# Another order of work at the opening of a three-layer kernel, and whole broadcasts of the group weights in place of pieces

## The reference

```python
x = x + 0.5 * ffn(layernorm(x)); x = x + attn(layernorm(x)); x = x + 0.5 * ffn(layernorm(x))

def ffn(x):                                   # 8 groups of 8 experts, inner width 352
    scores = softmax(x @ gate_w.T)            # 64 experts
    flat = w_e[:, inv_map]                    # the 8 best scores of each token, zero elsewhere
    scalar = flat.sum(-1)                     # one weight for each token and group
    soft = softmax(where(flat == 0, -1e9, flat), axis=-1)
    xg = x[:, None, :] + einsum('ngi,ghi->ngh', soft, mask_up_w)
    a = silu(einsum('ngh,gih->ngi', xg, gate_proj_w)) * einsum('ngh,gih->ngi', xg, up_proj_w)
    return einsum('ng,ngh->nh', scalar, einsum('ngi,ghi->ngh', a, down_proj_w))
```

## Time and profile before

| | |
|---|---|
| median of 3 runs | 1814.61 us |
| the profiled execution | 1818.04 us |
| its span, first to last instruction | 1816.3 us |
| PE busy | 1797.7 us, 99% |
| DVE busy | 876.9 us, 48% |
| ACT busy | 511.4 us, 28% |
| POOL busy | 174.2 us, 10% |
| moved by DMA | 384.13 MB, 211 GB/s on average |

### The profile page before, as it was taken

How to read it: one execution, slowest core, us unless ns; L and a number is a source line. 1 busy time by engine, 2 the same in 40 slices (tenths; PEclk the granted TensorE clock), 3 DMA queues, 4 the chain that set the end, 5 groups by cost and what they waited for, 6 DMA issues and landing times.

```text
span 1816.3 us, 21921 instructions
## 1 busy us (share of the span) xinstructions
PE 1797.7 (99%) x8320; PEld 1498.8 (83%) x8320; DVE 876.9 (48%) x1632; ACT 511.4 (28%) x754; POOL 174.2 (10%) x305
## 2 busy tenths in 40 slices
PE   7999999999999999999999999999999999999999
PEld 6888878888888888888888888888888888888887
DVE  6667454565445663343353656354664333422222
ACT  4334223532125431112212533114432111211111
POOL 2221210001100110000110101000101000000000
PEclk9999999999999999999999999999999999999999
DMA  5997765466465556567756556574466467656664
GB/s 202 366 354 261 278 228 170 159 200 209 139 220 199 173 185 197 184 235 236 243 182 203 190 189 225 166 236 160 155 203 219 145 237 255 223 173 229 234 232 167
DMA packets 108329, 384.13 MB, mean 211 GB/s; under 512 B 15520, under 2 KB 23584, under 8 KB 87488
## 3 DMA queue, kind: packets, MB, share of 16 engines
q1 hardware_dynamic: 65232, 278.36, 44.1%
q10 hardware_dynamic: 28816, 47.20, 9.1%
q0 software_dynamic: 14176, 57.16, 8.2%
HBM read 323.55 MB, written 41.81 MB: 201 GB/s over the span
## 4 chain that ended last, share of the span: by engine, by line
PE 92%; DMA 4%; DVE 2%; issue 0%; ACT 0%; SPq 0%; ACTq 0%; POOL 0%; DVEq 0%; POOLq 0%
PE bank L1243 27%; PE bank L1244 27%; PE bank L1245 27%; PE bank L1457 4%; DMA wt<-scr_w 2%; DMA b_all<-wgu 1%; PE bank L1396 1%; PE bank L1395 1%; PE bank L1388 1%; PE bank L1382 1%; DVE tb L865 1%; PE bank L1439 0%; PE bank L1438 0%; DVE o_all L860 0%; PE bank L1291 0%
## 5 line engine op out<-in xcount | busy, mean ns | idle before, releaser
L1243 PE MATMUL bank<-x_hi,wt 128*128 128x512 f32 x1328 | 521.0, 392 | 3.1 <-DMA wt<-scr_w 3.0
L1244 PE MATMUL bank<-x_hi,wt 128*128 128x512 f32 x1328 | 517.3, 390 | 0.0
L1245 PE MATMUL bank<-x_lo,wt 128*128 128x512 f32 x1328 | 517.3, 389 | 0.0
L808 DVE TENSOR_TENSOR act_t<-bank,sig 128x512 f32<-128x512 f32 x176 | 121.6, 691 | 514.9 <-PE bank L1457 473.9
L1243 PEld LDWEIGHTS bank<-x_hi,wt 128*128 128x128 f32 x1328 | 249.5, 188 | 55.4 <-DMA wt<-scr_w 4.8
L1245 PEld LDWEIGHTS bank<-x_lo,wt 128*128 128x128 f32 x1328 | 249.4, 188 | 52.0
L1244 PEld LDWEIGHTS bank<-x_hi,wt 128*128 128x128 f32 x1328 | 249.5, 188 | 50.3
L1243 PE MATMUL bank<-dt,a_hi 128*128 128x512 f32 x704 | 276.9, 393 | 0.8 <-issue 0.4
L1244 PE MATMUL bank<-dt,a_lo 128*128 128x512 f32 x704 | 274.4, 390 | 0.0
L1245 PE MATMUL bank<-dt,a_hi 128*128 128x512 f32 x704 | 274.2, 390 | 0.0
L722 ACT ACTIVATE sig<-bank 128x512 f32<-128x512 f32 x176 | 105.3, 598 | 559.7 <-PE bank L1457 559.6
(11 more groups left out here) (190 smaller groups left out, 1654.3 us busy)
## 6 DMA issues: line engine op xcount, KB each, us to landing
wt<-scr_w SPq DMA_DIRECT2D x140, 1152.0 KB, 5.2
dt<-scr_d SPq DMA_DIRECT2D x140, 512.0 KB, 5.3
s_bc<-scr_s ACTq DMA_DIRECT2D x128, 256.0 KB, 5.1
state<-wat POOLq DMA_DIRECT2D x28, 512.0 KB, 6.0
scr_w<-wt POOLq DMA_DIRECT2D x12, 1024.0 KB, 8.1
b_all<-wgu SPq DMA_DIRECT2D x22, 512.0 KB, 8.2
scr_d<-dt POOLq DMA_DIRECT2D x22, 512.0 KB, 5.0
x_lo<-tb SPq DMA_DIRECT2D x44, 256.0 KB, 5.1
```

The lines of the kernel that those rows point to most:

```text
L808: return nc.vector.tensor_tensor(dst, a, b, op)
L1243: mm(dst, wh, xh, start=start, stop=False)
L1244: mm(dst, wl, xh, start=False, stop=False)
L1245: return mm(dst, wh, xl, start=False, stop=stop)
```

## The change

Six things are done:

1. `first_norm` on ACT goes; `norm` on DVE normalises the first block's tiles too, with the same layout in memory as before. `first_scales` on POOL is replaced by `rstd_of`, and the shift is not computed. DVE's opening mixes statistics, normalisation and low parts.
2. The low part of gate_s moves from DVE to POOL.
3. `gu_hi(0)` and `gu_lo(0)` stand ahead of the masks' parts (mup); the preparation of fold_m stands ahead of the last `first_low`.
4. On PE, the first half of the gate sums of chunk 0 replaces the first half of `masked(0)` ahead of the fold; the second half of the sums follows the fold, then the whole of `masked(0)`.
5. `masked(4)` stands ahead of `down(0)`.
6. s_bc has two slots for each half of the groups. `load_s(half, m)` copies one group's row over all 128 partitions, 8 transfers in a phase where there were 28. A chunk that straddles two groups multiplies in parts, one for each group's partitions; a range from 32 to 128 is cut at 64. Over the 176 chunks that is 240 multiplications instead of 176.

```diff
-            def first_norm(i):
-                act.wait_ge(shift_ok, i + 1)
-                act.wait_ge(ld_x0[i], 16)
-                wait(act, xT_ok, i - 1)
-                nc.scalar.activation(xn[:, i % 2, :].rearrange("p (k d j) -> p k j d", k=KC, j=NQ),
-                                     xr(0)[:, i, :].rearrange("p (k j d) -> p k j d", k=KC, j=NQ), ACT.Identity,
-                                     bias=shift[:, i:i + 1], scale=rstd[:, i:i + 1]).then_inc(xn_ok, 1)
...
             def norm(r, i, src):
                 dve.wait_ge(mv_ok, r * NT + i + 1)
                 dve.wait_ge(rstd_ok, r * NT + i + 1)
+                if r == 0:
+                    wait(dve, xT_ok, i - 1)
+                    nc.vector.tensor_scalar(xn[:, i % 2, :].rearrange("p (k d j) -> p k j d", k=KC, j=NQ),
+                                            src[:, i, :].rearrange("p (k j d) -> p k j d", k=KC, j=NQ), mv[:, i, 0:1],
+                                            rstd[:, i:i + 1], ALU.subtract, ALU.mult).then_inc(xn_ok, 1)
+                    return
...
-            first_scales()
+            rstd_of(LN_R[0])
+            pool.wait_ge(gate_hi_ok, 1)
+            nc.gpsimd.tensor_tensor(gate_s[:, :, E:2 * E], raw_gate, gate_s[:, :, 0:E].bitcast(F32), ALU.subtract).then_inc(gate_ok, 1)
...
+            def s_number(n, g):
+                p, i = n // CH, g % (G // 2)
+                return p * (G // 2) + (G // 2 - 1 - i if p % 2 else i)
+            def s_last(n):
+                now = {s_number(n, g) for g, _, _ in group_rows(chunk(n))}
+                return sorted(now if n + 2 >= (n // CH + 1) * CH else now - {s_number(n + 2, g) for g, _, _ in group_rows(chunk(n + 2))})
+            def s_parts(c):
+                return [(g, a, b) for g, r0, r1 in group_rows(c) for a, b in (((32, 64), (64, P)) if (r0, r1) == (32, P) else ((r0, r1),))]
...
-            def load_s(n):
-                p, c = n // CH, chunk(n)
-                if n % CH < 2:
+            def load_s(half, m):
+                p, i = m // (G // 2), m % (G // 2)
+                if i == 0:
                     act.wait_ge(st_s, 16 * (p + 1))
-                for g, r0, r1 in group_rows(c):
-                    act.dma_start(s_bc[r0:r1, n % 2, :], scr_s[p % 2, g, :].partition_broadcast(r1 - r0)).then_inc(s_in[n % 2], 16)
+                g = half * (G // 2) + (G // 2 - 1 - i if p % 2 else i)
+                act.dma_start(s_bc[:, half, m % 2, :], scr_s[p % 2, g, :].partition_broadcast(P)).then_inc(s_in[half][m % 2], 16)
...
-                    if n + 2 < PHASES * CH:
-                        load_s(n + 2)
+                    for m in s_last(n):
+                        if m + 2 < PHASES * (G // 2):
+                            load_s(chunk(n) % 2, m + 2)
...
-                tt(act_t[:], s_bc[:, n % 2, :], act_t[:], ALU.mult).then_inc(t2_ok, 1)
+                for g, r0, r1 in s_parts(c):
+                    ins = tt(act_t[r0:r1, :], s_bc[r0:r1, c % 2, s_number(n, g) % 2, :], act_t[r0:r1, :], ALU.mult)
+                ins.then_inc(t2_ok, 1)
...
-            pe.wait_ge(setup_lo, 2)
-            masked(0, 0, KC // 2)
+            pe.wait_ge(gu_lo_ok, 1)
+            main(GB, 0, 0, 0, 0, KC // 2)
             pe.wait_ge(fold_ok, 1)
             router(0, 39)
-            masked(0, KC // 2, KC)
-            main(GB, 0, 0, 0)
+            main(GB, 0, 0, 0, KC // 2, KC)
+            pe.wait_ge(setup_lo, 2)
+            masked(0)
...
                     if n == 3:
+                        masked(4)
                         pe.wait_ge(sig_ok, 3)
                         pe.wait_ge(t1_ok, 3)
                         down(0)
-                        masked(4)
                         down(1)
```

More of the change, by code:

```diff
@@ L84, in build @@
         softT = sb("softT", [P, 2, 2, NB], F32R)
-        s_bc = sb("s_bc", [P, 2, NB])
+        s_bc = sb("s_bc", [P, 2, 2, NB])
         a_hi = sb("a_hi", [P, 2, NT, NQ, Q], F32R)
@@ L200, in build @@
         m_mm, m_raw_ok, m_top_ok, m_ok = (sem(n) for n in ("m_mm", "m_raw_ok", "m_top_ok", "m_ok"))
-        s_in, st_s = [sem(f"s_in{i}") for i in range(2)], sem("st_s")
+        s_in, st_s = [[sem(f"s_in{h}_{i}") for i in range(2)] for h in range(2)], sem("st_s")
         pool_init, setup_hi, setup_lo = (sem(n) for n in ("pool_init", "setup_hi", "setup_lo"))
@@ L424, in gu_lo @@
                                         ALU.subtract).then_inc(gu_lo_ok, 1)
[L426 to L436, removed]
             def store_w(c):
@@ L741, in _ @@
             act.dma_start(rank[:, 0, :], c_rank.partition_broadcast(P)).then_inc(ld_perm, 16)
[L742 to L743 removed]
             first_hi(0)
[L745 to L747 removed]
             act.wait_ge(ld_gate, 16)
             copy(gate_s[:, :, 0:E], raw_gate).then_inc(gate_hi_ok, 1)
+            first_hi(1)
             first_hi(2)
+            gu_hi(0)
             first_hi(3)
@@ L755, in _ @@
                      raw_mup[:, :, half, :].unsqueeze(2).broadcast_to([P, KC, 3, HE])).then_inc(setup_hi, 1)
-            gu_hi(0)
             gu_hi(1)
@@ L773, in _ @@
             m_top(1)
-            load_s(0)
+            for half in range(2):
+                load_s(half, 0)
             router(0, 49)
             router(0, 50)
-            load_s(1)
+            for half in range(2):
+                load_s(half, 1)
             for p in range(PHASES):
@@ L1150, in gate @@
                 dve.wait_ge(t1_ok, n + 1)
-                dve.wait_ge(s_in[n % 2], s_fill(n))
-                tt(act_t[:], s_bc[:, n % 2, :], act_t[:], ALU.mult).then_inc(t2_ok, 1)
+                c = chunk(n)
+                for g, _, _ in group_rows(c):
+                    m = s_number(n, g)
+                    dve.wait_ge(s_in[c % 2][m % 2], 16 * (m // 2 + 1))
+                for g, r0, r1 in s_parts(c):
+                    ins = tt(act_t[r0:r1, :], s_bc[r0:r1, c % 2, s_number(n, g) % 2, :], act_t[r0:r1, :], ALU.mult)
+                ins.then_inc(t2_ok, 1)
             def rest_a(n):
@@ L1169, in first_stats @@
                 stats_of(LN_R[0], i, xr(0))
-            for i in range(NT):
-                first_stats(i)
-            for i in range(NT):
-                first_low(i)
-                if i == 1:
-                    dve.wait_ge(gate_hi_ok, 1)
-                    tt(gate_s[:, :, E:2 * E], raw_gate, gate_s[:, :, 0:E].bitcast(F32), ALU.subtract).then_inc(gate_ok, 1)
-            dve.wait_ge(setup_hi, 2)
-            for half in range(2):
-                mp = mup[:, half, :, :].rearrange("p k (r e) -> p k r e", r=4)
-                tt(mp[:, :, 3, :], raw_mup[:, :, half, :], mp[:, :, 0, :].bitcast(F32), ALU.subtract).then_inc(setup_lo, 1)
-            gu_lo(0)
+            first_stats(0)
+            first_stats(1)
+            norm(LN_R[0], 0, xr(0))
+            first_stats(2)
+            norm(LN_R[0], 1, xr(0))
+            first_stats(3)
+            for i in range(NT - 1):
+                first_low(i)
+                if i < 2:
+                    norm(LN_R[0], i + 2, xr(0))
             dve.wait_ge(ld_perm, 48)
@@ L1191, in _ @@
             nc.vector.tensor_scalar(fold_m[:, E:2 * E], perm_w[:], iota[:, 0:1], None, ALU.is_equal).then_inc(fold_ok, 1)
+            first_low(NT - 1)
+            gu_lo(0)
+            dve.wait_ge(setup_hi, 2)
+            for half in range(2):
+                mp = mup[:, half, :, :].rearrange("p k (r e) -> p k r e", r=4)
+                tt(mp[:, :, 3, :], raw_mup[:, :, half, :], mp[:, :, 0, :].bitcast(F32), ALU.subtract).then_inc(setup_lo, 1)
             gu_lo(1)
@@ L1428, in weights, with masked @@
                 return hi, lo
-            def masked(c, k0=0, k1=KC):
+            def masked(c):
                 pe.wait_ge(gu_lo_ok, c + 1)
```

18 lines of the change are left out of this document (4 added, 14 removed).

## The result

The changed kernel takes 1818.7 us, the median of 20 executions (1816.15 to 1820.7), against 1814.92 for the kernel before (20 executions, 1813.36 to 1817.65). The ratio is 1.0017, with a 95% interval of 1.0011 to 1.0023: 2.0 to 4.2 us more, where 0.5 more was forecast and 1812.3 to 1817.4 was the range. The kernel is slower, by little: the ratio says 3.1 us, the medians 3.8, and the interval excludes that nothing changed.

A forecast was written before the change was run, and what follows sets the result against it. PE bounds the kernel, busy 1797.7 of 1816.3 us. Terms +0.9 (opening), +1.8 (masked(4)), -1.0 (77 us), -1.2 (weights) and 0 (multiplications) give +0.5 on the median 1814.6: 1815.1 us, range 1812.3 to 1817.4.

The forecast's parts named there:

- the two reliefs: PE's wait at 77.57 us and its waits for weights from scratch: forecast -1.0 and -1.2 us.
- step 1: Opening up to the fold, then the router's chain: PE stands from 33.8 to 35.5 us; cost +0.9 us.
- step 2: masked(4) ahead of down(0): PE waits for chunk 4's low weights from 47.54 to 49.94; +1.8 us, ends 0 and +2.0.
- The duration d: Opening: time of one tile's normalisation on DVE, taken as 1.1 us, with ends 0.55 and 1.29.
- the rival of the quick normalisation: Opening: DVE takes 0.55 to 0.7 us a tile, giving -1.0 instead of +0.9; 1813.2 us, chance 0.25.
- 9.0 + 4d: Opening: time in us when the fourth normalisation on DVE ends; 13.4 us with 1.1 us a tile.
- -1.0 at 77 us: PE's wait for sig of chunk 5 at 77.57 us disappears: -1.0 us, ends 0 and -1.0.
- -1.2 for the weights: PE's three waits for scratch weights: 0.7 off the longest, the other two gone; ends 0 and -3.0 us.
- the transfers were the whole cause: Rival: all 3.0 us of PE's waits for weights go, giving 1813.3 us; chance 0.10.
- The multiplications in parts: 64 more multiplications on DVE at straddling chunks: 44 us of DVE work hidden behind PE, cost 0.

The follow-up runs named there:

- the whole broadcasts alone: Kernel before with only the s_bc change: one group's row copied over all partitions per transfer, multiplications in parts; 1814.08 us, ratio 0.9995.

## Why the prediction was wrong

**Two steps failed: the price of a wait, and the two reliefs.** The first: step 1 ("stands until 35.5") and step 2 ("Cost: +1.8 us") price a stand of PE by the time in which it stands. The places and lengths were right: 1.89 us where 1.6 was said, 2.26 where 2.2 was. But a stand of this length in this place brings the clock down in part of the executions, and PE then does eight matmuls at half speed. In the 20 executions of the kernel after there are 7 x 1 + 9 x 2 = 25 falls, 1.25 each time, at 1.6 us: **2.0 us that no term holds**. The time goes up by 1.54 us from none to one fall and by 1.58 from one to two; in the five other versions of the table with executions of both kinds the difference is 0.7 to 2.0. Filling a wait removed the fall at its place and not at the other, in the one profile of each; filling both removed all, in eleven executions. The wait before route alone had a fall in 18 of 33 executions (8 + 5 + 5 of three kernels), the one ahead of `masked(4)` alone in 8 of 22, if every 0.999 there is a fall at the wait that was left. That two such waits near each other have more between them, 25 of 40, may be chance. The rows before the change could not have priced it: behind the one long wait inside the body of that kernel, 2.45 us, the clock stayed up. They could have raised the question, since all others were under 1 us, and the change makes two of about 2.

**The opening.** The duration d was 0.73 us, not 1.1; the rival of the quick normalisation came near with its 0.55 to 0.7. Here the mechanism was right and the term mis-sized: the fourth normalisation ends at 11.26 (9.0 + 4d gives 11.9), the fold starts at 17.07 (18.7 said), and DVE waits for the end of `masked(0)` in the middle of the router's chain, 1.19 us. That wait takes most of DVE's lead, which is 1.5 us ahead of it and 0.63 behind it; -0.4 us is left, and not +0.9. The prediction's own values, -1.0 for d = 0.55 and +0.9 for 1.1, give -0.4 in between for 0.73; that POOL's product sets the last of it was not in its chain. On its own row DVE does pay for the 16-byte spacing, 0.73 against 0.546 us, yet 0.2 where ACT pays 0.6. The Trainium skill's rule (SBUF — State Buffer, section Door 1: The DMA port swizzle), that each access which crosses to a new line costs a penalty, holds for both; the size is each engine's own.

**`masked(4)`.** +1.8 us was said, and by the marks +1.8 came, in the three profiles that have it without a fall. By the times it is 1.6 us between executions without a fall of the kernel after and of the one with it put back (1816.35 and 1814.78, two series), but only 0.4 where it alone was moved.

**The reliefs, the second step that failed.** -1.0 at 77 us and -1.2 for the weights came from waits of one profiled execution. They went, in the profile: both gone, the second with all 2.45 us, more than said. But that execution was 3.1 us above the median of its kernel, and two further profiles of it have neither wait. What isn't there can't be won: the whole broadcasts alone gave 0.9 us, with 0 in the interval, where the two reliefs were to bring 2.2. The prediction saw that the execution was "3.4 us above the median" and carried the difference over all the same; that was the mistake, since the waits for weights and at 77 us were 3.8 of its microseconds. The rival "the transfers were the whole cause" priced its gain from the same execution; its mechanism isn't borne out either, since six of the nine profiles with whole rows have waits for weights of 0.3 us or more.

**The multiplications in parts** cost nothing that shows: 240 instead of 176, DVE 48 us busier, and no new wait of PE on DVE in the attention phases.

**The sum by what was measured:** -0.4 for the opening, +1.8 for `masked(4)`, +2.0 for the falls, 0 to -0.9 for the broadcasts and what they relieve: +2.5 to +3.4, where the ratio says +3.1, the medians +3.8 and the interval +2.0 to +4.2. Without falls the kernel after is at 1816.35, 1.4 above before, which is -0.4 + 1.8. Against the forecast that is +2.0 for the falls, +1.3 to +2.2 for the reliefs that didn't come, and -1.3 for the opening. With the falls or the lost reliefs alone the time would have stayed within the range; the opening's error hid 1.3 us of both, and that was luck.

## What to carry to other kernels

Price a new wait of PE twice: by its length, and by what PE's clock does behind it; where a wait of about 2 us amid matmuls can't be avoided, put matmuls that have to be done anyway into it, even out of their order. Before a wait is counted as a gain, ask whether the profiled execution is a typical one: if it stands 3 us above the timed median and has 4 us of waits that hang on transfers, these are probably the 3 us. And look at the granted clock of each execution beside its time: here it sorted 20 scattered times into three groups that hardly overlap.

## What was not expected of the hardware

- A single wait of 1.9 to 2.3 us, after 10 us or more of unbroken matmuls, sufficed for the granted clock to fall to the 1.2 GHz level, with PE already at work again: in the profile of the kernel after it stood at 1.00 for about 1.4 us behind the wait before route, in another execution it was low from the first matmul. Over the eight falls in the profiles it began between 0.2 us ahead of PE's first matmul and 1.6 us behind it. The 2.45 us at 270 us in the kernel before, as long as they, left none behind them. The Trainium skill (TensorE: Matmul & The Clock Gate, section Part 1: The HAM clock gate) says of the slow matmuls at a kernel's start that the same kernel can show different numbers of them from run to run, since the chip's own watch isn't tied to the program's start. Of falls in the middle of a kernel these runs show the same scatter, with 4, 7 and 9 of 20 executions at none, one and two falls. That this is the reason is not shown here.
- In the opening the clock column doesn't tell the clock. It says 1.00 from 14 to 16 us in the kernel after, while matmuls of 256 columns start 0.21 us apart at 13.5 and 0.12 apart from 15.2 on, the two levels of the clock by their ratio. The same is seen in the kernel before, with the step at 15.8. The window, and then the timeline of PE:

```profile
14.00:16.00 2.00, 1.91 (x11) 1.73 (x11) 2.00 (x5) 1.03 (x2) 0.40 (x1) 1.00 0.06 24
```

```profile
13.50 0.41 PE L1273 MATMUL bank<-x_hi,gate_s 128*128 128x256 f32 x1
13.71 0.41 PE L1274 MATMUL bank<-x_lo,gate_s 128*128 128x256 f32 x1
...
15.34 0.28 PE L1274 MATMUL bank<-x_lo,gate_s 128*128 128x256 f32 x1
15.45 0.28 PE L1273 MATMUL bank<-x_hi,gate_s 128*128 128x256 f32 x1
```

- DVE's product of 32x256 elements took 0.42 us 21 times in each of the two kernels, and once 1.33 us after and 1.05 before. In every profile the long one ends 0.3 us after POOL's product beside it, whenever it began: starting 0.66 us earlier brought its end only 0.38 earlier.
- The waits for weights differ between executions of one kernel on work that doesn't differ: 3.0, 0.2 and 0 us in three profiles of before, 0, 0.8 and 0.3 in three of after. What sets them isn't settled. Nor is where the lower clock stood in the two executions of before that have 0.999: neither has a profile.
